# A fused feature network on one core: B halves of K tiles 1 to 3 handled whole instead of in column halves

## The reference

```python
w = jnp.einsum('bpf,mf->bpm', features, W_ft) + b_ft   # B 1024, p 2, f 5128, m 512
accumulator = stm * w
l1_x = jnp.clip(accumulator, 0.0, 1.0).reshape(features.shape[0], -1)
l2_x = jnp.clip(l1_x @ W1.T + b1, 0.0, 1.0)
return l2_x @ W2.T + b2
```

## Time and profile before

| | us |
|---|---|
| median of 3 runs | 396.63 |
| lowest and highest | 396.46 and 396.94 |
| the profiled execution's own time | 397.02 |
| its span on the core | 395.2 |
| TensorE busy, matmuls | 392.3 |
| VectorE busy | 347.3 |
| ScalarE busy | 197.8 |

### The profile page before, as it was taken

How to read it: one execution, slowest core, us unless ns; L and a number is a source line. 1 busy time by engine, 2 the same in 40 slices (tenths; PEclk the granted TensorE clock), 3 DMA queues, 4 the chain that set the end, 5 groups by cost and what they waited for, 6 DMA issues and landing times.

```text
span 395.2 us, 4882 instructions
## 1 busy us (share of the span) xinstructions
PE 392.3 (99%) x1863; PEld 323.9 (82%) x1863; DVE 347.3 (88%) x350; ACT 197.8 (50%) x209; POOL 14.6 (4%) x34
## 2 busy tenths in 40 slices
PE   9999999999999999999999999999999999999997
PEld 7888888888888888888888888888788888878886
DVE  5999999999999999999997788999787754999624
ACT  5565556643484433444334864344433447864500
POOL 0000044050000000000000000000000000000000
PEclk9999999999999999999999999999999999999999
DMA  8999989999966667766607689886567767674000
GB/s 285 389 390 392 390 300 361 310 282 231 336 242 225 226 245 265 252 222 229 229 0 264 227 304 400 333 307 251 182 238 260 257 230 231 232 248 134 0 2 2
DMA packets 43495, 97.85 MB, mean 248 GB/s; under 512 B 4072, under 2 KB 24816, under 8 KB 43152
## 3 DMA queue, kind: packets, MB, share of 16 engines
q1 hardware_dynamic: 42112, 95.18, 68.2%
q0 software_dynamic: 1072, 2.10, 1.8%
q10 hardware_dynamic: 288, 0.26, 0.2%
HBM read 96.87 MB, written 0.00 MB: 245 GB/s over the span
## 4 chain that ended last, share of the span: by engine, by line
PE 99%; DVE 0%; issue 0%
PE sums L617 94%; PE sums L697 3%; PE sums L723 1%; PE sums L735 1%; PE sums L713 0%; PE sums L731 0%; DVE res L548 0%; DVE hid L543 0%
## 5 line engine op out<-in xcount | busy, mean ns | idle before, releaser
L617 PE MATMUL sums<-x_hi,w_hi 128*128 128x512 f32 (+1 forms) x546 | 167.7, 390 | 0.0
L617 PE MATMUL sums<-x_hi,w_lo 128*128 128x512 f32 (+1 forms) x546 | 167.4, 389 | 0.0
L617 PEld LDWEIGHTS sums<-x_hi,w_hi 128*128 128x128 f32 x546 | 102.7, 189 | 21.7 <-issue 0.7
L617 PEld LDWEIGHTS sums<-x_hi,w_lo 128*128 128x128 f32 x546 | 102.8, 189 | 21.2
L617 PE MATMUL sums<-x_lo_home,w_hi 128*128 128x512 f32 (+1 forms) x386 | 119.2, 389 | 0.0
L371 ACT ACTIVATE x_hi<-xs 128x2048 fp32r<-128x2048 f32 x58 | 110.7, 1908 | 2.3 <-DVE xs L511 1.9
L366 ACT ACTIVATE w_hi<-ws 128x512 fp32r<-128x512 f32 x58 | 36.9, 635 | 146.8 <-PE sums L617 138.6
L520 DVE TENSOR_TENSOR x_lo_home<-xs,x_hi 128x2048 fp32r<-128x2048 f32 x40 | 91.4, 2285 | 12.9 <-ACT x_hi L371 12.9
L617 PEld LDWEIGHTS sums<-x_lo_home,w_hi 128*128 128x128 f32 x386 | 72.8, 189 | 14.9
L504 DVE TENSOR_TENSOR xs<-xs 128x2048 f32<-128x2048 f32 x20 | 45.7, 2284 | 0.0
L517 DVE TENSOR_TENSOR w_lo<-ws,w_hi 128x512 fp32r<-128x512 f32 x58 | 39.7, 685 | 6.3 <-ACT w_hi L366 6.2
(11 more groups left out here) (72 smaller groups left out, 198.6 us busy)
## 6 DMA issues: line engine op xcount, KB each, us to landing
xs<-x_p SPq DMA_DIRECT2D x40, 1024.0 KB, 5.2
xs<-x_p SPq DMA_DIRECT2D x56, 512.0 KB, 6.5
ws<-w_p SPq DMA_DIRECT2D x56, 256.0 KB, 2.8
ws<-w_p SPq DMA_DIRECT2D x44, 128.0 KB, 4.1
open_x<-x SPq DMA_DIRECT2D x5, 256.0 KB, 4.5
xr_raw<-x_rest POOLq DMA_DIRECT2D x1, 1024.0 KB, 7.8
stm_all<-stm SPq DMA_DIRECT2D x1, 1024.0 KB, 7.2
open_x<-x_p SPq DMA_DIRECT2D x1, 512.0 KB, 6.1
```

Source lines behind the costliest of these rows:

```text
L617: return nc.tensor.matmul(sums[:, bank, lo:hi], w[:, m * P:(m + 1) * P], x[:, c * BANK + lo:c * BANK + hi], start=start, stop=stop, skip_g ...
```

## The change

`pieces` gives two ranges to the B half of tile 0 alone, where it gave them to the B halves of tiles 0 to 3. The B halves (1,1), (2,1) and (3,1) now have the one range (0, 1024): one L490, one L354 and one L464 each, and one round of 12 products. `x_sums(g)` is adapted to this: with one sum for each tile and one more for tile 0, it is g + 2. The whole diff:

```diff
--- before.py
+++ after.py
@@ -229,7 +229,7 @@
         def pieces(g, pos):
             if (g, pos) == (0, 0):
                 return (0, HALF), (HALF, BANK), (BANK, COLS)
-            if (pos == 0 and g < 3) or (g < STAGED and pos == 1):
+            if (pos == 0 and g < 3) or (g, pos) == (0, 1):
                 return (0, BANK), (BANK, COLS)
             return ((0, COLS),)
 
@@ -240,7 +240,7 @@
             return lo_before(n) - 1
 
         def x_sums(g):
-            return g + 1 + min(g + 1, STAGED)
+            return g + 2
 
         def kept_count(g):
             f, k = pass_of(g)
```

## The result

| | before | after |
|---|---|---|
| median of 6 runs, us | 396.52 | 398.26 |
| lowest and highest | 396.32, 396.94 | 397.77, 398.89 |
| ratio, 95% interval | | 1.0043 [1.0032, 1.0054] |
| profiled execution, its own time | 397.02 | 398.62 |
| its span | 395.2 | 396.8 |

The change costs 1.74 us, beyond the 0.2% that a measurement can tell. First the page of the kernel after: its span, and the granted clock in 40 slices, which is the same row as before.

The account below looks back on a forecast made before the run. TensorE, almost never waiting, was taken to bound the kernel. Lost VectorE/ScalarE overlap, 0.73 us in each of three halves (2.19), opens a 1.07 us hole at (3,1): 396.63 + 1.07 = 397.7 us, range 397.1 to 398.5.

Parts of the forecast that it names:

- The hole: TensorE before (3,1), tile 3's B half: starts at 25.66 instead of 24.59 us, 1.07 us lost; chance 0.70 for 0.8 to 1.5.
- The 0.39 us taken off: Profiled execution lies 0.39 us above the median of 396.63, so 397.7 us was forecast instead of 398.09.
- a late start: VectorE's chain in the opening starting later costs in full; 0.4 us would give 398.1 us; no chance of its own.
- the early load: Rival: x of (0,1) lands in time, VectorE's chain starts up to 0.42 us sooner, hole 0.65, 397.3 us; chance 0.17.
- The restart: TensorE starting after a wait: 0.05 us to the weight load plus 0.10 for weights not loaded ahead, 0.15 us.
- The cover: VectorE's lead over TensorE's need in the opening of the kernel before: about 1.1 us.
- A second hole at (4,0): Low x of (4,0) usable at 30.20 us, TensorE wants it at 30.19: just fits, giving the same 1.07 us.
- The hole at (2,1): Tile 2's B half can start on TensorE at 21.85 us, wanted at 21.87: 0.02 us in time, no hole.
- The carried lag: Second pass, tile 22: 1.12 us of VectorE's lead gone, 1.76 of cover stay, price zero; rival 398.8 us, chance 0.03.
- The clock: Rival: after the hole TensorE falls from 2.4 to 1.2 GHz, 2.85 us more, 400.6 us; chance 0.04.
- Grouping: Rival: VectorE and ScalarE in series bound the kernel, fewer instructions save 0.96 us, 395.7 us; chance 0.03.
- SyncE: Load queues: SyncE waits on TensorE's progress only, so its waits move with TensorE.

Follow-up runs that it names:

- Sums ahead: The kernel after with only VectorE's order changed, sums one half ahead, all three halves whole: 396.76 us against 396.65 for the kernel before, ratio 1.0005.
- an equal lag in the kernel before: The kernel before with two extra 880-column subtractions on VectorE before the low x of (3,0), 2.19 us, column halves kept: 398.65 us, ratio 1.0055.
- The table: Four executions of the change, one with 21 warm-up products: 1.07 us plus both start offsets plus 0.08, against measured losses of 1.96, 1.74, 2.18 and 1.28 us.
- halves kept, sums ahead: VectorE's sums one half ahead, but with the column halves of the kernel before for (1,1), (2,1), (3,1): 397.13 us, 0.46 more than before, ratio 1.0014.
- the two later medians of the same kernel: The kernel with the change, unaltered, measured again and a third time: 398.61 and 398.58 us, ratios 1.0055 and 1.0052 against the kernel before.
- the second trace of the change: The kernel with the change run again, unaltered, for a second trace of its opening: 398.61 us, ratio 1.0055 against the kernel before.
- the third trace of the change: The kernel with the change run a third time, unaltered, for another trace of its opening: 398.58 us, ratio 1.0052 against the kernel before.
- the kernel before with 21 warm-ups: The kernel before with 21 instead of 17 warm-up products on TensorE: 396.60 us, 0.09 more than before, ratio 1.0005.

## Why the prediction was right, and its size too small

**Direction and mechanism: shown.** TensorE got waits on L354, VectorE three idle times before L464, of 0.79 us where I said about 0.7. The period is 3.82 us, I had 3.81. Sums ahead take the cost away, an equal lag in the kernel before brings it back.

**The hole: mis-sized, 1.07 us against 1.96 in the profile.** The failed step is the one in which I took both starting points, 15.25 us for VectorE and 24.59 us for TensorE's (3,1), from one execution as if they were properties of the kernel. The table shows them to be the execution's own. In ten traces with 17 warm-up products (3,0) starts between 15.60 and 16.59 us, and only one is later than the 16.43 that I had; L477 of (1,1), in those where nothing is put ahead of it, starts between 15.10 and 16.44, and only one is earlier than 15.25. In the seven other traces where both can be read, VectorE's later start and TensorE's earlier one add 0.6 to 1.1 us to the 1.07. That is why the runs of the change lie 1.7 to 2.0 us higher.

**The 0.39 us taken off.** The traces show what went wrong between the profiled execution and the median. Take an execution's own time and subtract the start of its (3,0) and what TensorE loses behind it, up to (4,1) and in the hole near 223 us of the last section. In all twelve traces 380.58 to 380.71 us are left (before: 397.02 - 16.43 = 380.59; after: 398.62 - 16.08 - 1.96 = 380.58; halves kept, sums ahead: 397.21 - 15.69 - 0.94 = 380.58). By this the execution traced for before, which loses nothing behind (3,0), lay 0.39 us above the median because its TensorE reached (3,0) late, and that lateness was cover. I took the 0.39 us off the time and kept the cover. Since VectorE's chain sets where (4,0) starts, the 398.09 us of the profiled execution needed nothing taken off; with the 0.08 us of the table it is 398.17, an estimate that takes VectorE's start from the one trace, against a measured 398.26.

I had named a late start as a possibility ("0.4 us would give 398.1 us"), but gave a chance of its own, 0.17, only to the early load. The range of 397.1 to 398.5 held 398.26; the two later medians of the same kernel, 398.61 and 398.58, lie just above it. The upper bound was too low.

**The restart: 0.15 us, measured 0.18.** From the end of L354 at 26.01 to the product is 0.06 us, and 0.12 us more pass in its group.

**The cover: about 1.1 us in the one trace, less in general.** By the medians, a lag of 0.73 us already costs 0.44, of 1.10 costs 0.76, of 1.46 costs 1.01 and of 2.19 costs 1.74 to 2.14: the lag less 0.05 to 0.45 us. The kernel before stands near the edge.

**A second hole at (4,0): not needed.** I had it fit by 0.01 us, and the profile shows 1.81 us for its two groups. The hole at (2,1), which I had miss by 0.02 us, opened, as it must with TensorE 0.35 us early and VectorE 0.47 us late.

**The carried lag.** The low x of tile 22 is there at 123.08 + 2.29 = 125.37 us and read at 127.29: 1.77 us of cover with 0.15 taken off, where I had 1.76. That rival is out.

**The clock.** After the holes the products keep 0.227 us (four in 0.907, 27.10 to 28.92 are eight in 1.82), the 2.4 GHz level, and the granted clock's row is unchanged. A hole of about 1.1 us did not bring the lower level back here. The Trainium skill (Perfetto Trace Analysis, "Optimizing Scalar/DVE Operations") says of engines that aren't saturated but make bubbles elsewhere that breaking instructions up may let work be completed sooner. The traces agree: with whole halves VectorE stands idle for 0.79 us in each period of 3.82, and TensorE has its holes; in the kernel before neither is there in these halves. The experiment with the sums ahead adds that whole instructions are as good when the order hides the hand-off.

**Grouping.** By the distances between starts a whole sum or low part saves VectorE 0.06 us (1.14 instead of 1.20). In the kernel after this is lost in its waiting. With the sums ahead it shows: 2.94 us for a half instead of 3.08.

**SyncE.** I wrote that its waits are on TensorE's progress only. The code has three that aren't: in the third pass (`TURN` on) it waits for VectorE's `x_sum` before two loads of operands and once more for `stm`. They cost nothing here: in the kernel after, TensorE waits for nothing between (3,1) and the head.

## What to carry to other kernels

Count a chain that goes back and forth between two engines as the sum of its steps as soon as both handle a tile whole, and as the longer engine's share only if another tile's work lies between. Before splitting instructions to get the overlap, see whether the order of whole ones can give it. And where a kernel's bound engine shows no wait, ask in several executions how much cover it had: a single trace gives the cover of that execution, and a change that uses it up will show the spread as time. If its time is corrected to the median, its cover has to be corrected with it.

## What was not expected of the hardware

The moment at which TensorE's products go from the lower to the upper level differs by execution, with the same instructions before it. In the trace of before 256 columns still took 0.215 us at 6.07 us; in the second trace of the change (3,0) stood 0.74 us earlier after the same start. The page's clock row shows neither. A late (3,0) can have another source: in the third trace of the change TensorE waited for ScalarE's L341 at 8.29 us and lost about 0.5 us there, which makes its (3,0), at 16.59 us, the latest of the ten.

A second, rarer hole of 0.38 us stands near 223 us, at the start of the third pass, in two of the twelve traces, one of a kernel with the change and one without. All engines, the kernel before with 21 warm-ups:

```profile
219.57 1.23 DVE L511 TENSOR_TENSOR xs<-xs 128x1024 f32<-128x1024 f32 x1 [1.18 <-DMA xs<-x_p]
...
220.83 1.92 ACT L371 ACTIVATE x_hi<-xs 128x2048 fp32r<-128x2048 f32 x1 [1.71 <-DVE xs L511]
...
222.66 2.04 ACT L398 ACTIVATE c_late<-sums 128x512 f32<-128x512 f32 x4
...
223.77 0.19 PEld L617 LDWEIGHTS sums<-x_hi,w_hi 128*128 128x128 f32 x1 [0.24 <-ACT c_late L398]
```

VectorE stood 1.18 us for a load of x (L511), ScalarE's rounding came 1.71 us late, the drain of the sums behind it too (L398, 222.66), and TensorE's weight load waited for that. In the trace of before the same L511 stood for no load. In these two executions 0.38 us of the time comes from there.
